# A hybrid convolution, attention and experts network on one core: group-norm preparation moved one stage earlier, and one block closed without GpSimd's drain

## What is computed

```python
# channel MLP of the first layer (end of _L0_conv_ref)
h2 = _ln(x, norm2_w, norm2_b)
h2 = jax.nn.gelu(h2 @ fc1_w + fc1_b, approximate=False)
x = x + (h2 @ fc2_w + fc2_b)

# Fourier layer: x = x + _L1_conv_ref(_gn(x), w1, w2, b1, b2)
def _gn(v, G=32, eps=1e-05):           # group norm: one mean and variance per image and group of 6 channels
    g = v.reshape(B_, H_, W_, G, C_ // G)
    m = jnp.mean(g, axis=(1, 2, 4), keepdims=True)
    s = jnp.var(g, axis=(1, 2, 4), keepdims=True)
    return ((g - m) / jnp.sqrt(s + eps)).reshape(v.shape)
xf = jnp.fft.rfft2(x, axes=(1, 2), norm='ortho')     # then two 24 x 24 block-diagonal complex layers,
o1r = xr @ w1[0] - xi @ w1[1] + b1[0]; ...           # each followed by softshrink, and
y = jnp.fft.irfft2(yf, s=(H, W), axes=(1, 2), norm='ortho') + bias

# two of eight experts for each token (_L2_ffn_ref)
h = jax.nn.silu(jnp.einsum('th,eih->tei', flat, w1))
outs = jnp.einsum('tei,ehi->teh', h, w2)             # only the two chosen experts are needed
combined = (sel * balanced[..., None]).sum(axis=1)
```

## Time and profile before

| | |
|---|---|
| median of three executions | 1156.06 us (1154.65 to 1159.53) |
| the profiled execution | 1155.44 us, of which 1153.6 us are the span of the trace |
| mean granted TensorE clock of that execution | 0.913 of full speed |
| TensorE busy | 998.3 us, 87% of the span |
| VectorE, ScalarE, GpSimd busy | 578.9, 420.4 and 286.6 us |

### The profile page before, as it was taken

The page is one execution under the profiler, slowest core; times in us unless marked ns, Lnnn a source line. Parts: engine busy times, 40 slices in busy tenths (PEclk is TensorE's granted clock), DMA queues, the critical chain, the costliest instruction groups (busy, mean ns, idle before and its releaser), DMA issues. The chain is left out here.

```text
span 1153.6 us, 20446 instructions
## 1 busy us (share of the span) xinstructions
PE 998.3 (87%) x7506; PEld 757.4 (66%) x7507; DVE 578.9 (50%) x1394; ACT 420.4 (36%) x853; POOL 286.6 (25%) x399
## 2 busy tenths in 40 slices
PE   6896999999699699899799839999929789993996
PEld 5685778787466488688699715666727545562775
DVE  3754554653311376465575654444448477844221
ACT  3665054546232133244352101111107356651332
POOL 4464320110100112100000262555422311103242
PEclk9885899999799899899998859999969899995899
DMA  8444863330002120200003711111133433415660
GB/s 92 118 120 122 163 159 81 81 82 2 1 28 71 43 63 2 55 1 1 2 1 84 227 34 30 49 48 49 40 109 90 124 118 99 141 54 173 201 204 15
DMA packets 103318, 91.58 MB, mean 79 GB/s; under 512 B 25905, under 2 KB 95095, under 8 KB 102590
## 3 DMA queue, kind: packets, MB, share of 16 engines
q1 hardware_dynamic: 93161, 77.15, 25.3%
q0 software_dynamic: 5632, 11.07, 3.6%
q10 hardware_dynamic: 4437, 2.17, 0.7%
HBM read 64.44 MB, written 29.70 MB: 82 GB/s over the span
## 5 line engine op out<-in xcount | busy, mean ns | idle before, releaser
L1305 DVE TENSOR_REDUCE l0a_nmax<-l0a_psS 98x2 f32<-98x392 f32 x96 | 54.4, 567 | 54.8 <-PE l0a_psS L1120 50.7
L2743 ACT ACTIVATE l2e_H<-l2e_psH 128x512 f32<-128x512 f32 x40 | 21.7, 594 | 130.2 <-PE l2e_psH L2705 130.2
L895 ACT ACTIVATE l3a_PT<-l3a_psST 128x512 f32<-128x512 f32 x96 | 54.6, 595 | 32.2 <-PE l3a_psST L806 31.4
L1255 ACT ACTIVATE l0a_PT<-l0a_psST 98x392 f32<-98x392 f32 x96 | 47.2, 497 | 42.2 <-PE l0a_psST L1162 41.9
L2723 PEld LDWEIGHTS l2e_psY<-W2T,l2e_HT 128*128 128x128 f32 x320 | 51.5, 190 | 15.9 <-issue 15.8
L2666 POOL DMA_INDIRECT ys<-l2e_Y,result_of x40 | 42.0, 1049 | 72.3 <-DVE l2e_Y L2770 66.2
L2723 PE MATMUL l2e_psY<-W2T,l2e_HT 128*128 x320 | 57.3, 332 | 1.3 <-DVE l2e_Y L2770 0.8
L941 DVE TENSOR_REDUCE l3a_nmax<-l3a_psS 128x2 f32<-128x512 f32 x48 | 33.0, 687 | 25.2 <-PE l3a_psS L776 25.2
L2770 DVE COPY l2e_Y<-l2e_psY 128x384 f32<-128x384 f32 x20 | 11.2, 558 | 65.2 <-PE l2e_psY L2723 65.2
L2702 PE MATMUL l2e_psH<-W1T,l2e_XT 128*128 x80 | 41.3, 640 | 2.7 <-issue 2.0
L2661 POOL DMA_INDIRECT l2e_X<-xn,token_at x40 | 39.3, 981 | 17.1 <-issue 17.1
(11 more groups left out here) (570 smaller groups left out, 2739.6 us busy)
## 6 DMA issues: line engine op xcount, KB each, us to landing
l3w_A<-in_w SPq DMA_DIRECT2D x8, 771.0 KB, 4.6
l3w_B<-in_w SPq DMA_DIRECT2D x8, 672.0 KB, 5.4
l3a_QS<-qd SPq DMA_DIRECT2D x72, 64.0 KB, 2.2
l3a_KS<-kd SPq DMA_DIRECT2D x72, 64.0 KB, 2.3
rd<-l0q_r_p SPq DMA_DIRECT2D x24, 168.0 KB
l0a_QS<-qd SPq DMA_DIRECT2D x54, 64.0 KB
l0a_KS<-kd SPq DMA_DIRECT2D x54, 64.0 KB
W2T<-in_w2t SPq DMA_DIRECT2D x2, 1536.0 KB, 16.7
```

What stands on the lines that cost most here:

```text
L895: nc.scalar.activation(PT[n % 3][:, s, :], psST[item % 2][:, :], ACT.Exp).then_inc(exp_done, 1)
L1255: ex = nc.scalar.activation(PT[n % 3][0:WQ, s, :], psST[item % 2][0:WQ, 0:2 * W0], ACT.Exp)
L1305: mx = nc.vector.tensor_reduce(nmax[k % 2][0:WQ, 2 * j:2 * (j + 1), s], psS[item % 2][0:WQ, 0:2 * W0].rearrange("p (t k) -> p t k", t=2), ...
```

## The change

It has two parts. The first makes a class `FourierFront`, whose buffers and semaphores (`l1g_`) live through the channel MLP's stage and the Fourier stage. The block weights' clearing, their 20 DMAs and the negation, the constant rows, and the whole group norm of pair 0 are issued in the channel MLP's stage, on the same engines as before; pairs 1 to 3 call the same methods at the same places as before.

```diff
 class Stage:
-    def block(self):
-        return self.ctx.enter_context(self.nc.Block())
+    def block(self, drained=True):
+        return self.ctx.enter_context(self.nc.Block(no_gpsimd_drain=not drained))

+class FourierFront:
+    def clear_weights(self):
+        self.nc.gpsimd.memset(self.W1[:], 0.0).then_inc(self.w_zeroed, 1)
+        self.nc.gpsimd.memset(self.W2[:], 0.0).then_inc(self.w_zeroed, 1)
+        self.nc.gpsimd.memset(self.lam[:, :], -LAMBDA).then_inc(self.negated, 1)
+    def load_weights(self, sp, w):
+        sp.wait_ge(self.w_zeroed, 2)
...
+    def mean(self, pe, psM, p):
+        pe.wait_ge(self.sum_done, 2 * p + 2)
...
+        self.nc.tensor.matmul(psM[:, 0:2 * GROUPS], self.ones[:, :], ...).then_inc(self.mean_mm, 1)
+    def total(self, dve, p, *ready):
+        for sem, value in ready:
+            dve.wait_ge(sem, value)
...

-def l0_mlp(nc, G, w):
+def l0_mlp(nc, G, w, gn, w_next):
         def _(sp):
+            gn.load_weights(sp, w_next)
             for p in range(NP - 1):
         def _(pool):
+            gn.clear_weights()
             for p in range(NP):
                 nc.gpsimd.tensor_tensor(X, X, free(b2[:, 0:1], [0, 4], [1, C]), ALU.add).then_inc(x_biased, 1)
+                if p == 1:
+                    gn.negate_weights(pool)
         def _(pe):
                 first(p)
                 if p + 1 < NP:
                     norm(p + 1)
+                if p == NP - 2:
+                    pe.wait_ge(xT_done, 2 * NP)
+                    gn.mean(pe, psT[0], 0)
+                if p == NP - 1:
+                    gn.variance(pe, psT[1], 0)
                 second(p)
         def _(act):
                 hidden(p)
                 if p + 1 < NP:
                     norm(p + 1)
+                if p == NP - 2:
+                    gn.square(act, 0)
+                    gn.square(act, 1)
+            gn.root(act, 0)
         def _(dve):
                 if p + 1 < NP:
                     norm(p + 1)
+                if p == NP - 2:
+                    gn.total(dve, 0, (x_in, 16))
+                    gn.centre(dve, psT[0], 0)
+                if p == NP - 1:
+                    gn.square_total(dve, 0)
+                    gn.with_eps(dve, psT[1], 0)
+                    gn.scale(dve, 0)
+                    gn.norm(dve, 0)
                 for a in range(2):
...
+                if p == 0:
+                    gn.constant_rows()

-def experts_any(nc, G, transfers, rows_out):
+def experts_any(nc, G, transfers, rows_in, rows_out):
-        x_in = [st.sem(f"x_in{r}") for r in range(RING)]
-        y_out = rows_out
+        x_in, y_out = rows_in, rows_out
-        block = st.block()
+        block = st.block(drained=False)
```

More of the change, by code:

```diff
@@ L1494, in afno_tiles, with l1_afno @@
     return [(t["ones"], consts["gnones"]), (t["DF"], consts["dft"]), (t["IV"], consts["idft"]), (t["IVB"], consts["idftb"])]
-def l1_afno(nc, G, w, consts, transfers):
+def l1_afno(nc, G, w, consts, transfers, gn):
     with Stage(nc, "l1") as st:
         NP, R = B // 2, CH + 1
+        W1, W2, lam, FX, C1, negated = gn.W1, gn.W2, gn.lam, gn.FX, gn.C1, gn.negated
         ones, DF, IV, IVB = (G["afno"][n] for n in ("ones", "DF", "IV", "IVB"))
-        W1 = st.sb("W1", [R, 2, 3, CH])
-        W2 = st.sb("W2", [R, 2, 3, CH])
-        lam = st.sb("lam", [CH, 1])
         two = lambda name, shape: [st.sb(f"{name}{u}", shape) for u in range(2)]
[L1510 to L1513, removed]
+        XN, XS, xn_done = gn.XN, two("XS", [P, TI, C]), gn.xn_done
         UP, DN = two("UP", [CH, 2, 2 * NF]), two("DN", [CH, 2, 2 * NF])
@@ L1582, in _ @@
         def _(pe):
[L1583 to L1593, removed]
             def forward(i):
@@ L1648, in backward @@
                 mm.then_inc(y_mm, 1)
-            mean(0)
-            variance(0)
             for p in range(NP):
@@ L1655, in _ @@
                 if p + 1 < NP:
-                    mean(p + 1)
+                    gn.mean(pe, psM, p + 1)
                 first(2 * p)
@@ L1659, in _ @@
                 if p + 1 < NP:
-                    variance(p + 1)
+                    gn.variance(pe, psV, p + 1)
                 second(2 * p)
@@ L1695, in _ @@
             act.wait_ge(negated, 1)
-            act.wait_ge(zeroed, Z)
-            square(0)
-            square(1)
-            root(0)
+            act.wait_ge(gn.rows_set, 4)
             for p in range(NP):
@@ L1710, in _ @@
                 if p + 1 < NP:
-                    root(p + 1)
+                    gn.root(act, p + 1)
         @block.vector
@@ L1758, in norm @@
-            def norm(p):
-                for u in range(2):
-                    i = 2 * p + u
-                    if p:
-                        dve.wait_ge(f_mm, 2 * i - 2)
-                        dve.wait_ge(xs_done, i - 1)
-                    V.tensor_tensor(in_groups(XN[u][:]), in_groups(XC[u][:]), spread(rstd[:, u, 0:1]), ALU.mult).then_inc(xn_done, 1)
             def hidden(i, a):
@@ L3296, in build @@
         net.window_attention()
-        net.window_mlp()
-        net.fourier()
+        with Stage(nc, "l1g") as across:
+            gn = FourierFront(across, net.G)
+            net.window_mlp(gn)
+            net.fourier(gn)
         net.landmark_attention()
         with Stage(nc, "l2y") as between:
-            rows_out = [between.sem(f"rows_out{r}") for r in range(RING)]
-            net.two_experts(rows_out)
+            rows_in, rows_out = ([between.sem(f"{name}{r}") for r in range(RING)] for name in ("rows_in", "rows_out"))
+            net.two_experts(rows_in, rows_out)
             with Stage(nc, "l3f") as across:
```

189 lines of the change are left out of this document (103 added, 86 removed).

## The result

The changed kernel takes 1144.66 us, the median of four runs (1142.76 to 1146.19), against 1156.58 for the kernel before on the same chip: a ratio of 0.990, 95% interval 0.988 to 0.992. Measured a second time it took 1144.11 (ratio 0.989, 0.987 to 0.991). The forecast was 1141.0, range 1137.5 to 1147.5, faster with a chance of 0.93. So the direction and the range held, but of the 14.9 us of the sum some 12 arrived.

What follows compares the result with a forecast made beforehand. TensorE, busy 87% of the span, was taken to bound the kernel, with long holes at the Fourier head and experts' end; 9.2 + 5.7 = 14.9 us off the median 1156.06 gave 1141 us, range 1137.5 to 1147.5.

Steps and rivals of the forecast that it cites:

- the sum: Whole kernel: gains of 9.2 us at the Fourier stage's head and 5.7 at the experts' end add to 14.9 us.
- The Fourier head: Start of the Fourier stage: pair 0's group norm moves into the channel MLP; gain 9.2 us, bounds 6.4 to 10.3.
- the mean's wait: Channel MLP: the mean ahead of pair 2's second layer waits for ScalarE's reading of pair 3's turned tiles; +1.7 us.
- the joint: Channel MLP to Fourier stage: the first transform matmul starts 0.47 us after VectorE's last addition.
- the transform: Fourier stage: pair 0's 16 matmuls take 4.12 us instead of 5.92, ending at 393.6 instead of 402.76.
- the memsets: Channel MLP's start: two GpSimd memsets beside VectorE's first eight pieces cost +0.65 us, bounds 0 and 1.2.
- a full lock: Channel MLP's start: GpSimd's memsets block VectorE entirely through shared SBUF interfaces; cost 1.2 us, the sum 0.5 us worse.
- rival C: Channel MLP: pair 0's sums wait for tokens back from DRAM, one us per us past 361; chance 0.03.
- The experts' block: End of the two-of-eight experts: leaving out GpSimd's drain removes the 6.6 us idle; gain 5.7 us, bounds 0 to 6.2.
- rival A: Experts' end: the meeting waits for something besides the drain, or GpSimd stays occupied with puts; 5.7 us missing; chance 0.11.
- rival B: Fourier head gains only 5.4 us, through a longer TensorE wait or a clock fall; about 1145 us; chance 0.08.
- the forecast's own range: Whole kernel: 1138.5 to 1144 us if both parts work as forecast, chance 0.78.

## Why the prediction was right, and where it was not

The Fourier head: right, 9.9 us measured against 9.2. Depending on which two profiles are compared it is 8.8 to 10.5, since the stretch took 96.50 and 96.68 us in the two with the old head and 86.19 to 87.71 in the six with this same new one. The parts: the mean's wait cost 1.62 (1.7 said), the joint 0.32, not 0.47, the transform 4.09 (4.12), and the memsets 0.30, not 0.65, since four of the eight pieces took 0.52 to 0.65 us instead of 0.31 to 0.38, but the pieces overlap on VectorE and the last one started only 0.30 later. Two of the long pieces ended at 308.34 and 308.44, just behind the first memset (308.29), the other two at 309.00 and 309.10, just behind the second (308.95), so VectorE seems to have waited for them and made up most of it. The Trainium skill, "GPSIMD Engine Reference", "Key points", speaks of shared SBUF interfaces; the pieces are longer beside the memsets, but the stage by only 0.30 us for 1.4 us of memsets, and not by the 1.2 that the prediction works out for a full lock. The trip through DRAM (rival C) was never near: pair 0's sums were done at 354.67, 7.9 us before the mean.

The experts' block: right, 5.9 against 5.7, and rival A is dead. One sentence of its working was wrong: that no row shows the drain. One did, in the view of the block's own line in the kernel before, which counts the sequencers' instructions too (ns, least, median, most):

```profile
L77 POOLq DRAIN  x12: 34/880/8575, 110.3 to 1149.7; - x12
```

This largest one runs from 842.0 to 850.6, just before the next stage starts; read beforehand, it would have spoken strongly against rival A. The Trainium skill, "VectorE: DVE Perf Modes", "The DRAIN you can't avoid", has some 12 ns for the drains of a program's preamble and postamble, on all five engines. Of drains at a block's end in between it says nothing: here GpSimd's took from 34 ns to 8.57 us, the longest behind 80 indirect DMAs.

The step that failed is the sum: 9.2 + 5.7 were taken off the end as if all behind them moved as one. Between the two changed stretches the same 2712 matmuls took 3.1 us more of TensorE's time, with 6.9 us more at a granted clock of 0.50. The prediction put such a loss at nothing without a reason. It had the clock in the changed stretch alone (rival B, which did not come). 1155.44 - 15.8 is 1139.6; with the 3.1, and 1.6 net of the other unchanged stretches, the 1144.88 follow but for 0.5 that lies outside the span. In the medians the same: 11.9 of 15.8.

That the range held is in part luck. 1144.66 lies outside the forecast's own range (1138.5 to 1144) and beside rival B's 1145, but not by B's mechanism: the mean's wait and the transform were as forecast. The range reached that far only to take in A and B. And why TensorE spends more of the unchanged stretch at 0.50 in most executions with the shorter head stays open.

## What to carry to other kernels

Count on a shift only as far as the next place where TensorE has little to do: behind it the same matmuls can cost some microseconds more or less, by where the granted clock falls. Look for GpSimd's drain in the rows of the block's own line wherever a block issues indirect DMAs, and let it come where GpSimd has slack. A new wait on the busiest engine was cheaper here inside its next group of matmuls than ahead of it (0.28 instead of 1.62 us).

## What was not expected

GpSimd's drain costs some 0.082 us per indirect DMA since its last drain, 47 us after the landing too (80 DMAs more in both comparisons). Unchanged stretches scatter a lot: the start up to the channel MLP took 303.65 to 309.23 us in fourteen profiles (mean granted clock 0.91 in the shortest, 0.90 in the longest), and one of some 440 us spread over 5. And idle matmuls that kept the clock up gave 3.4 us in their stage, while the full attention behind it took 1.6 to 4.6 us longer in these two profiles than in the twelve others.
